# The second layer norm's scale and shift moved from ScalarE to GpSimd, beside a split of matrix operands on VectorE

## The chip, the cores and the metric

One core of one Trainium2 chip runs the whole program. The metric is the device time of one execution in microseconds, the median over several runs. The core's engines work side by side, each through its own list of instructions in order, and meet by semaphores: TensorE (PE; its weight loads are PEld), VectorE (DVE), ScalarE (ACT), GpSimd (POOL) and SyncE (SP, which here only issues DMAs).

## The reference, cut to what matters

The input `x` is 32 graphs of 256 nodes with 128 features. There are two residual blocks, each with a layer norm and a maximum with zero ahead of it:

```
h = jnp.maximum(_layernorm(x, axis=-1), 0.0)
x = x + _L0_gnn_ref(h, adj, W, a)                 # graph attention (GAT)
h = jnp.maximum(_layernorm(x, axis=-1), 0.0)      # the norm that the change is about
x = x + _L1_gnn_ref(h, adj, ...)                  # GCN, then LSTMs over windows of 1 to 4 nodes
...
# in _L1_gnn_ref
h = relu(einsum('ts,bsh->bth', adj, x @ Wg0 + bg0))
h = relu(einsum('ts,bsh->bth', adj, h @ Wg1 + bg1))
for p in range(1, 5):                             # LSTM over windows of p nodes
    last = _lstm_last(Wih[p-1], Whh[p-1], bih[p-1], bhh[p-1], windows of p nodes)
    h = h with node p*i + p-1 replaced by last[i]
```

All of it is float32. Layer norm is `(x - mean) / sqrt(var + 1e-5)` over the features. The kernel forms a scale and a shift for each node from the node's mean and variance, so that the norm is `x * scale + shift`.

## The kernel before, in words

The 32 graphs are worked as 16 pairs; a pair is 512 nodes, four tiles of 128 nodes (partitions) by 128 features. Everything stays in SBUF: `xs` holds all tiles.

There are three stages, each a software pipeline written out by hand. `ticks` runs a body once per tick and gives each step of the body its own pair (`live(s)` says whether step s has a pair in this tick).

Stage A (`phase_a`, 16 pairs) is the GAT. Stage B (`phase_b`) is the GCN and the LSTM for p = 1; its first four ticks run beside the last ticks of stage A. After it come the `ROUNDS`, the LSTMs for p = 2, 3 and 4, and the output.

In stage B, TensorE's products are exact float32 products made of three matmuls each: an operand is split in a high part (rounded to the type fp32r) and a low part (the rest), and `hi*hi + lo*hi + hi*lo` is summed (`product`, L1044). Each step therefore needs a split between two products: ScalarE writes the high part of what lies in PSUM (`part_hi`, L600), VectorE the low part (`part_lo`, L820 or L822). The steps of one pair are:

- step 0: the normed tile is written to `v_norm` by ScalarE (`second_norm`, L510: four activations with Relu, one per tile, scale and bias per node); VectorE splits it (`s_hi[0]` by a copy, L834, and `s_lo[0]` by a subtraction, L836).
- step 1: twelve matmuls with the adjacency matrix (`adjT`); step 2: four with `wg0` and the bias (the last is L1114); step 3: three with `wg1`; then ScalarE adds a bias (`y1`, L607) and TensorE turns the result with four transposes (`turned`, L1090) for step 4: twelve matmuls with `adjP`.
- step 5: nine matmuls for the three LSTM gates; ScalarE's sigmoids and tanh (L583, L576), VectorE's cell products (L796 to L807).

In one tick TensorE goes through steps 5, 4, 3, 2, the transposes, and 1. ScalarE goes through tanh, the gates I, G and O, `part_hi(4)`, `y1`, `part_hi(2)`, `part_hi(3)`, `second_norm`, `part_hi(1)`. The gate O waits until VectorE has read the row that it overwrites (L796). VectorE goes through L796, L800, L804, L807, `part_lo(4)`, `part_lo(2)`, `part_lo(3)`, the split of step 0 (L834, L836), `part_lo(1)`.

`second_norm(t)` may overwrite `v_norm` when VectorE has split the pair before (`b_lo[0]` at t). The first of them is issued in tick 16 of stage A, as soon as TensorE has turned the last tile of the first norm, which uses the same `v_norm`.

GpSimd computes the scales and shifts in chunks of 16 tiles (`norm_scale`, L407 to L416, whose power L415 is the longest instruction): four chunks for the second norm, each when VectorE has taken that chunk's statistics. Then it splits the LSTM weights for p = 2 to 4 in twelve pieces of two instructions each (`split_weights`, L474 and L475), one or two per tick: each piece waits for `one_lo`, VectorE's L807 in a tick of stage B. TensorE and ScalarE wait for all pieces (`wl_ok` at 2) before the LSTMs of p = 2.

Of the kernel before, what the change touches and what calls it, by code (L numbers as in the profile page):

```python
# [5 lines left out]
def preln_gat_gcn_lstm_kernel(  # L6
# [22 lines left out]
    fp32 = mybir.dt.float32  # L29
    fp32r = mybir.dt.float32r  # L30
    ALU = mybir.AluOpType
# [6 lines left out]
    PAIRS = B // 2  # L38
# [11 lines left out]
    SKIPS = 4  # L50
# [8 lines left out]
    with ctx:  # L59
# [7 lines left out]
        xs = sb("xs", [P, TILES, D])  # L67
# [314 lines left out]
        def _(pool):  # L382
# [88 lines left out]
            def split_weights(p, m, c):  # L471
                i, j = (p - 1) // 2, (p - 1) % 2
                g = slice(c * 2 * D, (c + 1) * 2 * D)
                done(nc.gpsimd.tensor_copy(wl_of[0][i][:, j, m, g], wraw[:, m, p - 1, g]))  # L474
                done(nc.gpsimd.tensor_tensor(wl_of[1][i][:, j, m, g], wraw[:, m, p - 1, g],  # L475
                                             wl_of[0][i][:, j, m, g].bitcast(fp32), ALU.subtract))
# [4 lines left out]
            split_weights(1, 0, 1)  # L481
            nc.gpsimd.nop().then_inc(wl_ok, 1)

            for c in range(4):
                pool.wait_ge(stats_ok, TILES + (c + 1) * QUARTER)
                norm_scale(1, c * QUARTER, QUARTER)


            for n_, (p, m, c) in enumerate((p, m, c) for p in range(2, SKIPS + 1) for m in range(2) for c in range(2)):
                pool.wait_ge(one_lo, 1 + 3 * n_ // 4)  # L490
                split_weights(p, m, c)
            nc.gpsimd.nop().then_inc(wl_ok, 1)

        @block.scalar
        def _(act):
# [56 lines left out]
                    nc.scalar.activation(pT[:, :, :].rearrange("p k i -> p (k i)"),  # L552
                                         psPT.rearrange("p b n -> p (b n)"), ACT.Copy).then_inc(a_pT, 1)

            def second_norm(t):
                act.wait_ge(ln_ok, t + (PAIRS + 1))
                normalise(1, t, range(4), b_v)

            def phase_a(t, ph, live):
                behind = (t - 1, ph - 1, lambda s: live(s + 1))  # L560
                early_a(*behind)
                first_norm(t, ph, live)
                if isinstance(t, int) and t == PAIRS:
                    act.wait_ge(a_T, PAIRS)
                    second_norm(0)
                late_a(*behind)
                if isinstance(t, int) and t == 4:
                    act.wait_ge(rs_ps, 1)
                    nc.scalar.activation(rs_raw[:, :], ps[:, 7, 0:N], ACT.Copy).then_inc(rs_read, 1)

            act.wait_ge(ones_ok, 1)
            def phase_b(t, ph, live):
                if live(6):

                    act.wait_ge(one_cell, t - 5)
                    nc.scalar.activation(one_row(R_TC), one_row(R_C), ACT.Tanh).then_inc(one_act, 1)  # L576
                if live(5):

                    for j, g in enumerate((I, G, O)):
                        act.wait_ge(one_gate, t * 3 + (j + 1 - 15))  # L580
                        if g == O:
                            after(act, one_h, t - 5, 0)
                        nc.scalar.activation(one_row(g), ps[:, 4 + g, :], ACT.Tanh if g == G else ACT.Sigmoid,  # L583
                                             bias=bl[:, g:g + 1]).then_inc(one_act, 1)

                def part_hi(s):
                    if not live(s):
                        return
                    if s == 4:
                        dst = h_hi[:, bass.ds((t - 4) * PN, PN)]  # L590
                    else:
                        dst = s_hi[:, s, :]
                    if s == 3:

                        act.wait_ge(b_T, t - 2)
                    else:
                        act.wait_ge(b_mm[s], t - s + 1)
                    if s < 4:
                        after(act, b_mm[s + 1], t - s, 0)
                    nc.scalar.activation(dst, ps[:, TURNED if s == 3 else s - 1, :],  # L600
                                         ACT.Copy if s in (1, 3) else ACT.Relu).then_inc(b_hi[s], 1)

                part_hi(4)
                if live(3):
                    act.wait_ge(b_mm[3], t - 2)
                    after(act, b_T, t - 3, 0)
                    nc.scalar.activation(y1[:, :], ps[:, 2, :], ACT.Identity, bias=b1_col[:, 0:1]).then_inc(b_y, 1)  # L607
                part_hi(2)
                part_hi(3)
                if live(0) and not (isinstance(t, int) and t == 0):  # L610

                    act.wait_ge(b_lo[0], t)
                    second_norm(t)
                part_hi(1)

            ticks(act, 5, 4, phase_a, beside=phase_b, lag=1)
# [52 lines left out]
        def _(dve):  # L669
# [115 lines left out]
            def phase_b(t, ph, live):  # L785
# [43 lines left out]
                if live(0):  # L829

                    v = v_norm[:, :, :].rearrange("p k f -> p (k f)")
                    dve.wait_ge(b_v, t + 1)
                    after(dve, b_mm[1], t, 0)
                    nc.vector.tensor_copy(s_hi[:, 0, :], v).then_inc(b_hi[0], 1)  # L834
                    dve.wait_ge(b_hi[0], t + 1)
                    nc.vector.tensor_tensor(s_lo[:, 0, :], v, s_hi[:, 0, :].bitcast(fp32),  # L836
                                            ALU.subtract).then_inc(b_lo[0], 1)
                part_lo(1)

            ticks(dve, 5, 4, phase_a, beside=phase_b)  # L840
# [412 lines left out]
```

## Time and profile before

| | us |
|---|---|
| median of 3 runs | 450.65 (450.28 to 450.68) |
| the profiled execution | 451.49 |
| span of its instructions | 449.5 |
| PE busy in the span | 426.2 (95%) |
| DVE busy | 376.1 (84%) |
| ACT busy | 333.6 (74%) |
| POOL busy | 67.3 (15%) |

The times are of whole executions; the span is that of the instructions of the one execution that the profiler recorded. Busy time adds up the instructions' own durations. A matmul's duration is longer than the distance to the next one, since matmuls are pipelined, so PE's idle time is read from the starts of neighbouring matmuls and from what the profile says they waited for. Stage A ends, beside the first ticks of stage B, at about 112 us of the span; stage B alone runs to about 226 us.

### The profile page before, as it was taken

The page shows a single profiled execution, that of the slowest core. Times are in us where ns is not written, and L with a number is a line of the kernel's source. Part 1 is how long each engine was busy: PE and PEld are TensorE (multiplying, and loading weights), DVE is VectorE, ACT ScalarE, POOL GpSimd, SP SyncE. Part 2 cuts the span into 40 slices and gives each one's busy share as a digit, 9 for nine tenths or more (in the row PEclk, how much of TensorE's full clock was granted, in tenths as well). Part 3 has the DMA queues.
Part 4 walks back from the last instruction along what each step waited for, and adds up shares of the span by engine and source line. Part 5 has one row for each costly group of instructions (what it writes and reads, how often), then busy time and mean ns, then how long its engine had stood idle before and what let it go on. Part 6 is the DMA issues. An engine that isn't in the chain of part 4 may idle for free.

```text
span 449.5 us, 7890 instructions
## 1 busy us (share of the span) xinstructions
PE 426.2 (95%) x2472; PEld 369.0 (82%) x2472; DVE 376.1 (84%) x994; ACT 333.6 (74%) x651; POOL 67.3 (15%) x145
## 2 busy tenths in 40 slices
PE   5689999979999999999999999999999999999995
PEld 4468788878888888888778888899999988887884
DVE  5999999987778787877778888878888789888995
ACT  3779999966899999897787768667767675574552
POOL 3678442240411313100000000000000000000000
PEclk9989999989999999999999999999999999999999
DMA  8910000000000000000000000000000000002116
GB/s 244 335 56 1 1 3 0 0 1 0 2 0 2 0 0 0 0 0 0 1 1 1 0 1 1 0 2 0 1 1 1 2 0 0 1 23 71 47 47 188
DMA packets 14212, 11.67 MB, mean 26 GB/s; under 512 B 1123, under 2 KB 12390, under 8 KB 13926
## 3 DMA queue, kind: packets, MB, share of 16 engines
q1 hardware_dynamic: 12118, 10.11, 7.5%
q10 hardware_dynamic: 2064, 1.18, 1.0%
q8 instruction: 16, 0.26, 0.2%
q14 instruction: 14, 0.11, 0.1%
HBM read 7.10 MB, written 4.19 MB: 25 GB/s over the span
## 4 chain that ended last, share of the span: by engine, by line
PE 69%; DVE 21%; ACT 4%; issue 3%; DMA 1%; DVEq 1%; POOL 0%; ACTq 0%; POOLq 0%
PE ps L1044 45%; PE ps L1188 12%; PE ps L1192 6%; DVE score L760 5%; DVE score L726 4%; DVE xs L774 3%; DVE stats L675 2%; PE ps L1090 2%; DVE stats L716 2%; ACT v_norm L510 1%; PE ps L1024 1%; ACT work L635 1%; PE ps L1135 1%; DMA xs<-in_x 1%; PE ps L1114 1%
## 5 line engine op out<-in xcount | busy, mean ns | idle before, releaser
L635 ACT ACTIVATE work<-ps,bl 128x512 f32<-128x512 f32 (+2 forms) x204 | 111.1, 628 | 26.9 <-PE ps L1192 19.3
L1044 PE MATMUL ps<-h_hi,wl_hi 128*128 128x512 f32 (+3 forms) x252 | 93.5, 371 | 0.9 <-DVE xs L916 0.8
L1044 PE MATMUL ps<-h_hi,wl_lo 128*128 128x512 f32 (+3 forms) x252 | 92.8, 368 | 0.0
L1044 PE MATMUL ps<-h_lo,wl_hi 128*128 128x512 f32 (+3 forms) x252 | 92.7, 368 | 0.0
L625 ACT ACTIVATE work<-work 128x512 f32<-128x512 f32 (+2 forms) x56 | 31.5, 571 | 45.1 <-DVE work L911 34.6
L510 ACT ACTIVATE v_norm<-xs,shift,scale 128x128 f32 (+1 forms) x128 | 52.7, 490 | 2.6 <-POOL shift L425 2.6
L1044 PEld LDWEIGHTS ps<-h_hi,wl_hi 128*128 128x128 f32 x252 | 47.5, 188 | 8.3 <-issue 1.2
L1044 PEld LDWEIGHTS ps<-h_lo,wl_hi 128*128 128x128 f32 x252 | 47.4, 188 | 6.6
L1044 PEld LDWEIGHTS ps<-h_hi,wl_lo 128*128 128x128 f32 x252 | 47.5, 188 | 5.6
L1188 PE MATMUL ps<-s_hi,wl_hi 128*128 128x512 f32 (+2 forms) x144 | 51.7, 362 | 0.0
L1188 PE MATMUL ps<-s_hi,wl_lo 128*128 128x512 f32 (+2 forms) x144 | 51.2, 358 | 0.0
L1024 PE MATMUL ps<-wh,pT 128*128 128x130 f32 x256 | 34.2, 288 | 2.4 <-DVE xs L774 2.1
L583 ACT ACTIVATE work<-ps,bl 128x512 f32<-128x512 f32 x48 | 30.9, 685 | 6.4 <-DVE work L796 5.1
L1024 PEld LDWEIGHTS ps<-wh,pT 128*128 128x128 f32 x256 | 31.4, 198 | 4.9 <-ACT pT L552 3.3
L1192 PE MATMUL ps<-s_lo,wl_hi 128*128 128x512 f32 (+2 forms) x144 | 34.4, 358 | 0.3 <-DVE s_lo L873 0.3
L600 ACT ACTIVATE s_hi<-ps 128x512 fp32r<-128x512 f32 x48 | 28.2, 593 | 5.5 <-PE ps L1114 2.1
L862 DVE TENSOR_TENSOR s_hi<-work 128x512 fp32r<-128x512 f32 (+2 forms) x36 | 22.0, 610 | 12.0 <-ACT work L625 11.1
L543 ACT ACTIVATE prob<-score,ebias 128x256 f32<-128x256 f32 x64 | 27.4, 512 | 5.7 <-DVE ebias L738 5.7
L866 DVE TENSOR_TENSOR work<-work 128x512 f32<-128x512 f32 (+2 forms) x52 | 31.3, 602 | 0.0
L1188 PEld LDWEIGHTS ps<-s_hi,wl_hi 128*128 128x128 f32 x144 | 27.1, 188 | 3.0
L1188 PEld LDWEIGHTS ps<-s_hi,wl_lo 128*128 128x128 f32 x144 | 27.1, 188 | 2.9
L1192 PEld LDWEIGHTS ps<-s_lo,wl_hi 128*128 128x128 f32 x144 | 25.4, 188 | 3.8 <-DVE s_lo L873 0.6
(136 smaller groups left out, 911.7 us busy)
## 6 DMA issues: line engine op xcount, KB each, us to landing
result<-xs SPq DMA_DIRECT2D x12, 256.0 KB, 2.3
work<-in_w_ih_t SPq DMA_DIRECT2D x1, 1024.0 KB, 10.4
work<-in_w_hh_t SPq DMA_DIRECT2D x1, 1024.0 KB, 9.4
xs<-in_x SPq DMA_DIRECT2D x2, 256.0 KB, 3.8
xs<-in_x SPq DMA_DIRECT2D x1, 512.0 KB, 7.2
result<-xs SPq DMA_DIRECT2D x4, 128.0 KB, 2.5
result<-xs ACTq DMA_DIRECT2D x4, 128.0 KB, 2.8
adj_raw<-in_adj ACTq DMA_DIRECT2D x1, 256.0 KB, 6.8
```

The lines of the kernel that those rows point to most:

```text
L510: ins = nc.scalar.activation(v_norm[:, k, :], xs[:, bass.ds(i, 1), :].rearrange("p o f -> p (o f)"), ACT.Relu, scale=scale[:, which, bass. ...
L543: ins = nc.scalar.activation(prob[:, m, k], score[:, m, k], ACT.Exp, scale=1.0 - SLOPE, bias=ebias[:, m, k:k + 1])
L583: nc.scalar.activation(one_row(g), ps[:, 4 + g, :], ACT.Tanh if g == G else ACT.Sigmoid, bias=bl[:, g:g + 1]).then_inc(one_act, 1)
L600: nc.scalar.activation(dst, ps[:, TURNED if s == 3 else s - 1, :], ACT.Copy if s in (1, 3) else ACT.Relu).then_inc(b_hi[s], 1)
L625: nc.scalar.activation(lw[:, par, R_TC, 0:cols], lw[:, par, R_C, 0:cols], ACT.Tanh).then_inc(c_act[par], 1)
L635: nc.scalar.activation(lw[:, par, g, 0:cols], ps[:, 4 * par + g, 0:cols], ACT.Tanh if g == G else ACT.Sigmoid, bias=bl[:, (p - 1) * GATES ...
L760: ins = nc.vector.scalar_tensor_tensor(score[:, m, k], psS[:, b * N:(b + 1) * N], wh[:, m, k, D + 1:D + 2], score[:, m, k], ALU.max, ALU.add)
L866: nc.vector.tensor_tensor(row(r, par, R_H), row(r, par, O), row(r, par, R_TC), ALU.mult).then_inc(c_h[par], 1)
L1024: ins = nc.tensor.matmul(psA[:, b, ui * (D + 2):(ui + 1) * (D + 2)], pT[:, 2 * b + uj, ui * P:(ui + 1) * P], wh[:, (ph - 4) % 4, 2 * b + u ...
L1044: ins = nc.tensor.matmul(dst, a, b, start=start and n_ == 0, stop=stop and n_ == 2)
L1188: nc.tensor.matmul(ps[:, 4 * par + g, 0:cols], part, s_hi[:, par, 0:cols], start=False, stop=False)
L1192: nc.tensor.matmul(ps[:, 4 * par + g, 0:cols], weights(p, 1, g)[0], s_lo[:, par, 0:cols], start=False, stop=True).then_inc(c_gate[par], 1)
```

## The change: what it does

The four activations of `second_norm` go from ScalarE's list to GpSimd's, as four `tensor_scalar` instructions (multiply by the scale, add the shift) without the maximum with zero. VectorE's split takes the maximum on: the copy (L834) becomes a `tensor_scalar` with a maximum, the subtraction (L836) a `scalar_tensor_tensor` that takes the maximum and then subtracts. GpSimd waits for the same two events as ScalarE did (the last transposes of the first norm for pair 0, `b_lo[0]` for the others), and for no scale but its own.

GpSimd's list changes its order with it: the first two chunks of scales, then the pairs' norms one by one, the third chunk after pair 4 and the fourth after pair 6; the twelve pieces of the LSTM weights follow the norms of pairs 7 to 15 (two after pairs 7, 10 and 13, one after the others), and their own waits for `one_lo` are gone.

```diff
@@ -481,14 +481,33 @@
             split_weights(1, 0, 1)
             nc.gpsimd.nop().then_inc(wl_ok, 1)
 
-            for c in range(4):
+            def second_scale(c):
                 pool.wait_ge(stats_ok, TILES + (c + 1) * QUARTER)
                 norm_scale(1, c * QUARTER, QUARTER)
 
-            for n_, (p, m, c) in enumerate((p, m, c) for p in range(2, SKIPS + 1) for m in range(2) for c in range(2)):
-                pool.wait_ge(one_lo, 1 + 3 * n_ // 4)
-                split_weights(p, m, c)
+            def second_norm(q):
+                if q == 0:
+                    pool.wait_ge(a_T, PAIRS)
+                else:
+                    pool.wait_ge(b_lo[0], q)
+                for k in range(4):
+                    i = q * 4 + k
+                    ins = nc.gpsimd.tensor_scalar(v_norm[:, k, :], xs[:, i, :], scale[:, 1, i:i + 1], shift[:, 1, i:i + 1],
+                                                  ALU.mult, ALU.add)
+                ins.then_inc(b_v, 1)
+            second_scale(0)
+            second_scale(1)
+            pieces = [(p, m, c) for p in range(2, SKIPS + 1) for m in range(2) for c in range(2)]
+            for q in range(PAIRS):
+                second_norm(q)
+                if q in (4, 6):
+                    second_scale(q // 2)
+                for n_, piece in enumerate(pieces):
+                    if 7 + 3 * n_ // 4 == q:
+                        split_weights(*piece)
             nc.gpsimd.nop().then_inc(wl_ok, 1)
 
         @block.scalar
@@ -552,17 +571,10 @@
                     nc.scalar.activation(pT[:, :, :].rearrange("p k i -> p (k i)"),
                                          psPT.rearrange("p b n -> p (b n)"), ACT.Copy).then_inc(a_pT, 1)
 
-            def second_norm(t):
-                act.wait_ge(ln_ok, t + (PAIRS + 1))
-                normalise(1, t, range(4), b_v)
             def phase_a(t, ph, live):
                 behind = (t - 1, ph - 1, lambda s: live(s + 1))
                 early_a(*behind)
                 first_norm(t, ph, live)
-                if isinstance(t, int) and t == PAIRS:
-                    act.wait_ge(a_T, PAIRS)
-                    second_norm(0)
                 late_a(*behind)
                 if isinstance(t, int) and t == 4:
                     act.wait_ge(rs_ps, 1)
@@ -607,10 +619,6 @@
                     nc.scalar.activation(y1[:, :], ps[:, 2, :], ACT.Identity, bias=b1_col[:, 0:1]).then_inc(b_y, 1)
                 part_hi(2)
                 part_hi(3)
-                if live(0) and not (isinstance(t, int) and t == 0):
-                    act.wait_ge(b_lo[0], t)
-                    second_norm(t)
                 part_hi(1)
 
             ticks(act, 5, 4, phase_a, beside=phase_b, lag=1)
@@ -831,10 +839,10 @@
                     v = v_norm[:, :, :].rearrange("p k f -> p (k f)")
                     dve.wait_ge(b_v, t + 1)
                     after(dve, b_mm[1], t, 0)
-                    nc.vector.tensor_copy(s_hi[:, 0, :], v).then_inc(b_hi[0], 1)
+                    nc.vector.tensor_scalar(s_hi[:, 0, :], v, 0.0, None, ALU.max).then_inc(b_hi[0], 1)
                     dve.wait_ge(b_hi[0], t + 1)
-                    nc.vector.tensor_tensor(s_lo[:, 0, :], v, s_hi[:, 0, :].bitcast(fp32),
-                                            ALU.subtract).then_inc(b_lo[0], 1)
+                    nc.vector.scalar_tensor_tensor(s_lo[:, 0, :], v, 0.0, s_hi[:, 0, :].bitcast(fp32), ALU.max,
+                                                   ALU.subtract).then_inc(b_lo[0], 1)
                 part_lo(1)
 
             ticks(dve, 5, 4, phase_a, beside=phase_b)
```

## Rows read from the trace of the kernel before

**Rows 1.** Windows: length; busy us (instructions) of PE, PEld, DVE, ACT, POOL; clock.
```profile
84.30:89.30 5.00, 5.00 (x40) 4.34 (x39) 5.00 (x24) 5.00 (x13) 0.00 (x0) 1.00 0.00 0
...
132.74:205.31 72.57, 72.21 (x441) 61.85 (x441) 59.95 (x121) 66.42 (x131) 13.57 (x24) 1.00 0.00 0
205.31:212.38 7.07, 7.07 (x44) 6.18 (x45) 5.49 (x11) 5.33 (x9) 0.00 (x0) 1.00 0.00 0
```

**Rows 2.** Chain that ended last, 84 to 130 us: start, us, what.
```profile
107.58 1.65 ACT v_norm L510 x4
...
119.08 1.65 ACT v_norm L510 x4
```

**Rows 3.** Timeline of PE, first ticks of stage B: start, duration, what [idle before].
```profile
105.87 0.47 PE L1044 MATMUL ps<-s_hi,wg_hi 128*128 128x512 f32 x1 [0.38 <-issue]
...
110.58 0.40 PE L1044 MATMUL ps<-s_lo,wg_hi 128*128 128x512 f32 x1
111.16 0.47 PE L1044 MATMUL ps<-s_hi,wg_hi 128*128 128x512 f32 x1 [0.18 <-DVE s_lo L820]
...
116.34 0.39 PE L1044 MATMUL ps<-s_lo,wg_hi 128*128 128x512 f32 x1
116.90 0.47 PE L1044 MATMUL ps<-s_hi,wg_hi 128*128 128x512 f32 x1 [0.17 <-DVE s_lo L820]
...
124.67 0.40 PE L1114 MATMUL ps<-rs_parts,b_parts 128*128 128x512 f32 x1
125.49 0.66 PE L1090 MATMUL ps<-ident,y 128*128 128x128 f32 x4 [0.42 <-ACT y L607]
```

**Rows 4.** Timeline around the transposes, in a tick with and one without second_norm.
```profile
146.50 0.69 ACT L607 ACTIVATE y<-ps,b_col 128x512 f32<-128x512 f32 x1
146.82 0.40 PE L1114 MATMUL ps<-rs_parts,b_parts 128*128 128x512 f32 x1
147.25 0.66 PE L1090 MATMUL ps<-ident,y 128*128 128x128 f32 x4
...
211.63 0.69 ACT L607 ACTIVATE y<-ps,b_col 128x512 f32<-128x512 f32 x1
212.13 0.40 PE L1114 MATMUL ps<-rs_parts,b_parts 128*128 128x512 f32 x1
212.38 0.66 PE L1090 MATMUL ps<-ident,y 128*128 128x128 f32 x4
```

**Rows 5.** Groups on POOL by line and shape: busy us, mean ns.
```profile
L475 POOL TENSOR_TENSOR wl_lo<-work,wl_hi 128x256 fp32r<-128x256 f32 x14 | 10.3, 739 | 1.1
L474 POOL CAST wl_hi<-work 128x256 fp32r<-128x256 f32 x14 | 5.6, 398 | 54.6 <-DVE h_lo L807 54.2 <-POOL adjP_lo L466 0.2
L411 POOL TENSOR_SCALAR ln_d<-ln_d 128x16 f32<-128x16 f32 x7 | 1.9, 271 | 0.4
...
L448 POOL CAST ident_r<-ident 128x128 fp32r<-128x128 f32 x1 | 0.3, 291 | 0.0
```

**Rows 6.** Timeline of DVE in a steady tick of stage B.
```profile
150.11 0.43 DVE L834 CAST s_hi<-v_norm 128x512 fp32r<-128x512 f32 x1 [0.85 <-ACT v_norm L510]
150.58 0.69 DVE L836 TENSOR_TENSOR s_lo<-v_norm,s_hi 128x512 fp32r<-128x512 f32 x1
...
151.79 0.82 DVE L796 TENSOR_TENSOR work<-work 128x176 f32<-128x176 f32 x3
```

**Rows 7.** Timeline of ACT in the same tick, gate O.
```profile
152.70 0.69 ACT L583 ACTIVATE work<-ps,bl 128x512 f32<-128x512 f32 x1 [0.46 <-DVE work L796]
```

**Rows 8.** Timelines of DVE and POOL where their instructions overlap.
```profile
97.06 0.69 DVE L836 TENSOR_TENSOR s_lo<-v_norm,s_hi 128x512 fp32r<-128x512 f32 x1
97.15 0.67 POOL L411 TENSOR_SCALAR ln_d<-ln_d 128x16 f32<-128x16 f32 x1
...
119.72 2.91 POOL L415 TENSOR_TENSOR scale<-ln_a,half 128x16 f32<-128x16 f32 x1
121.22 0.69 DVE L836 TENSOR_TENSOR s_lo<-v_norm,s_hi 128x512 fp32r<-128x512 f32 x1
```

## The prediction

> **What bounds the kernel now.** I read the windows first, then the chain of waits, then the timelines of TensorE, ScalarE and VectorE around what the chain named.
>
> In the windows [rows 1] the reader is to see who is full where. In stage A alone VectorE is: 5.00 of 5.00 us of a tick. In stage B TensorE is: 72.21 of 72.57 us in ten ticks, while ScalarE has 66.42 and VectorE 59.95. The first window takes part of this change off ScalarE at no gain: the norm of pair 0 is issued there, and VectorE sets that pace.
>
> The three windows also hold an experiment that the old kernel makes by itself. A steady tick takes 72.57 / 10 = 7.257 us. The tick of 205.31 to 212.38 does the same 44 matmuls but has no norm left to do, since its pair would be the seventeenth: 7.07 us. The difference is 0.18 us. It sits in one place [rows 4]: with the norm, the transposes (L1090) start 147.25 - 146.82 = 0.43 us after the matmul before them, without it 212.38 - 212.13 = 0.25 us. What they wait for is `y` (L607), which starts 0.32 us ahead of that matmul with the norm and 0.50 us ahead without.
>
> In the first ticks of stage B the norm is on the chain itself [rows 2]: 1.65 us in each of three ticks (first and last are shown, the third is at 113.33). TensorE, though, stands still for much less than that there, because it still has stage A's matmuls to fill in [rows 3].
>
> **The change, part by part.**
>
> *Off ScalarE.* Four activations in each of 16 pairs go, 1.65 us per pair [rows 2], about 26 us of ScalarE in all. As ScalarE is not full, only what TensorE waits for counts.
>
> First ticks: TensorE's stalls that hang on the norm [rows 3]. At 105.87 it had stood 0.38 us; the low part that it wants comes from VectorE behind the split, which sat waiting for the norm. At 111.16 it starts 0.58 us after the matmul before, at 116.90 0.56 us after; with 0.25 us for an unhindered distance (the one of the free tick [rows 4]) that is 0.33 and 0.31 us lost, both on the same low part. At 125.49 the distance is 0.82 us, so 0.57 lost, on `y`, in the tick in which ScalarE has to do the norm, a table load and three gates one after the other. Sum: 0.38 + 0.33 + 0.31 + 0.57 = 1.6 us. What is late next there is TensorE itself: without these stalls its matmuls follow each other.
>
> Steady ticks: from the transposes at 125.49 [rows 3] to those at 205.31 [rows 1] are 79.82 us, 11 ticks of 7.256. Each can fall to 7.07: 11 x 0.18 = 2.0 us. What comes next is TensorE again, and a tick cannot go below its own matmuls.
>
> Does VectorE let `y` come earlier? The free tick had no split to do, the changed ticks still have, so VectorE's dates have to be looked at. The split (L834) now sits idle 0.85 us for the norm [rows 6]; L796 follows it in order, and gate O, which waits 0.46 us for L796 [rows 7], is followed by `part_hi(4)` and `y`. So if GpSimd's norm is there in time, L796 and O move up by as much as 0.85 us, where `y` needs 0.18. VectorE may lose 0.85 - 0.18 = 0.67 us ahead of L796 before the first of the gain is gone.
>
> *On GpSimd.* Four `tensor_scalar` of 128x128 with a scalar per partition. The trace has none of them. Below: the one-input copy of the same size, 0.29 us; above: the two-input subtraction of twice the size, 0.74 us [rows 5]. I take 0.3, by the nearest in size and number of inputs; a norm is then 1.2 us, at the upper end 3.0 us. It starts when the split (L836) of the pair before ends, 150.58 + 0.69 = 151.27 in the tick shown, and is wanted at the next tick's split, 7.07 us after 150.11 - 0.85 = 149.26 [rows 6], thus at 156.33: 5.1 us of room. Even 3.0 us fit, so the cost is nothing on the path; cover ends at 1.27 us per instruction. Pair 0's norm falls into stage A, and its split is reached only just ahead of 97.06 [rows 8].
>
> *Scales in between.* A chunk is 2.91 us [rows 8] and nine small instructions of 0.27 (L411's mean [rows 5], which includes slow ones), so 5.3 us. It runs behind the norms of pairs 4 and 6, whose successors then start at most some 1.2 + 5.3 = 6.5 us after the last, under a tick: nothing on the path.
>
> *Weight pieces.* A piece is 0.398 + 0.739 = 1.14 us [rows 5], twelve of them in nine ticks, now behind the norm: 1.2 + 1.14 = 2.3 us, or 3.5 with two. Both are under a tick, and the last is done behind pair 15's norm, some five ticks ahead of the LSTMs that wait for it. No DMA is moved, and no queue is passed by one.
>
> *VectorE's split.* The copy at 0.43 us becomes a `tensor_scalar`; bounds are that and the 0.69 us of the two-input form [rows 6]; I take 0.43, as it has still one tensor input. The subtraction stays at 0.69, with the same inputs. At the upper bound VectorE does 0.26 us more per tick and has 7.07 - 59.95 / 10 = 1.07 idle, and 0.67 ahead of L796: nothing either way.
>
> *What GpSimd and VectorE do to each other.* This is the unknown. Until now GpSimd's pieces ran where VectorE reads PSUM; now norm and pieces run behind L836, into the row L796, L800, L804, L807, all from SBUF: 0.82 + 0.43 + 0.69 + 0.69 = 2.6 us, the last three by their likes in [rows 6]. The trace has two such meetings [rows 8]. L411, issued 0.09 us after L836, took 0.67 us instead of its mean of 0.27 [rows 5]: GpSimd waited. And L836 at 121.22, 1.5 us into a GpSimd instruction of 2.91, took its 0.69 us as everywhere: VectorE did not wait. So I take nothing for VectorE and up to the whole row, 2.6 us, for GpSimd: norm plus that is 3.8 of the 5.1 us of room. The other bound, VectorE waiting for all of it, is the second rival.
>
> The Trainium skill, "SBUF — State Buffer", section "SBUF: two separate sides", says that the two engines share a port pair under an exclusive lock: whichever instruction starts first holds it to its end, and the other is blocked fully. The first meeting agrees; the second speaks against it, as L836 would have had to wait until 119.72 + 2.91 = 122.63, though that instruction reads only 16 columns. By the rule the sum would be the second rival's.
>
> **Sum.** 1.6 + 2.0 = 3.6 us. The profiled execution took 451.49 us, span 449.5 and 1.99 around it: 445.9 and 447.9 after. It lay 0.84 above the median of the runs; on the median, 450.65 - 3.6 = 447.05, so **447.0**. Nothing behind 212 us is touched, so the gain is handed on to the end.
>
> **Rivals.**
>
> 1. *Only the first ticks gain.* VectorE or GpSimd's port costs some 0.2 to 0.8 us ahead of L796, `y` stays as late as it was, and the steady ticks stay at 7.26. For it: VectorE's row has little air before L796. Against: 0.67 us are free. Time: 450.65 - 1.6 = 449.05.
>
> 2. *VectorE is held up by GpSimd and becomes the bound (slower).* Place: the nine ticks with weight pieces. Of the norm's four instructions the first two fall beside `part_lo(1)`, which reads PSUM; the other two and the piece hold the port against VectorE for 0.6 + 1.14 = 1.74 us, with two pieces 2.88. VectorE has 1.07 free per tick at the new pace, so six ticks lengthen by 0.67 and three by 1.81: 9.4 us, against 3.6 gained: 456.5 at the full hold. It decides from about 70% of these durations, where the loss is 6 x 0.15 + 3 x 0.95 = 3.7 and eats the gain; under 37% nothing is lost. Half-way between 70 and 100% it is 6 x 0.41 + 3 x 1.38 = 6.6 lost: 453.7. For it: the norm runs just where VectorE reads two SBUF operands. Against: the second meeting in [rows 8]. The rule of the Trainium skill's page "SBUF — State Buffer" named above comes to this rival.
>
> 3. *No difference.* GpSimd's norm is late, above 1.27 us per instruction or with its waits on VectorE, and VectorE waits at the split as before, for another engine: about 450.6. For it: that instruction isn't in the trace. Against: it would have to be four times its nearest row.
>
> **How the numbers follow.** The forecast has 0.60, with its own range of 446.2 to 447.7 (the stalls of [rows 3] may come back in part, the small ones beside them may go too). Rival 1 has 0.18, rival 2 0.14, rival 3 0.08. About 0.2%, 0.9 us, is what a measurement of this kernel can tell from no change. Faster: 0.60 + 0.18 = 0.78; same 0.08; slower 0.14. The range goes from 446.0 to 450.2, which takes in rival 1 and partial forms of the others.
>
> **What would show it.** Right: the transposes of stage B 0.25 us behind the matmul before them and ticks of 7.07; L834 without idle time for the norm; `tensor_scalar` on GpSimd near 0.3 us, longer where it lies beside L796 to L807; stage B's first transposes of a full tick (125.49) some 1.6 us earlier. Wrong: L796, L804, L807 longer than now or with idle time that ends with GpSimd; ticks with two pieces longer than ticks with one; L834 still waiting, now for GpSimd; or the `tensor_scalar` on VectorE at 0.69 us.

## The result, and the profile after

The changed kernel's median is 445.79 us (444.55 to 446.20, 5 runs); the kernel before had 450.28 us beside it (448.84 to 450.68). The ratio is 0.9895 (95% interval 0.9871 to 0.9919): faster by about 1%. The forecast was 447.0 us in a range of 446.0 to 450.2: right in direction, and the median lies 0.2 us below the range.

The profiled execution took 444.66 us. Its span of 442.9 is 6.6 us less than that of the profiled execution before. That is more than the medians differ by (4.5 us), so the 6.6 us are taken apart first. Lines of the changed kernel are eight higher from the edit on: L1052 was L1044, L1098 (the transposes) L1090, L1122 L1114, L496 is GpSimd's norm, L842 and L844 are the split. Kernels of the experiments have their own line numbers; the names of the tiles tell which instruction a line is.

Windows of the changed kernel, columns as in [rows 1]: a tick of stage A alone, one tick of stage B, then ten.

```profile
84.30:89.30 5.00, 5.00 (x41) 4.34 (x40) 5.00 (x25) 4.47 (x10) 1.75 (x4) 1.00 0.00 0
...
114.02:121.10 7.08, 7.08 (x46) 6.19 (x45) 4.39 (x7) 5.97 (x9) 6.45 (x13) 1.00 0.01 2
...
128.17:198.90 70.73, 70.73 (x441) 61.87 (x441) 60.82 (x120) 53.64 (x90) 47.92 (x69) 1.00 0.00 0
```

The ten ticks take 70.73 us against 72.57 in [rows 1], with the same 441 matmuls, and TensorE is now busy in all of it. ScalarE went from 66.42 to 53.64, GpSimd from 13.57 to 47.92. In stage A VectorE is still the full one: ScalarE's release there bought nothing.

TensorE's timeline in the first ticks of stage B, to be laid beside [rows 3]. The distance from one start to the next is what counts.

```profile
101.86 1.04 PE L1044 MATMUL ps<-ident,prob 128*128 128x128 f32 x8
102.65 0.48 PE L1052 MATMUL ps<-s_hi,wg_hi 128*128 128x512 f32 x1
...
107.35 0.40 PE L1052 MATMUL ps<-s_lo,wg_hi 128*128 128x512 f32 x1
107.58 0.40 PE L1052 MATMUL ps<-s_hi,wg_hi 128*128 128x512 f32 x1
...
110.40 0.28 PE L1052 MATMUL ps<-adjT_lo,s_hi 128*128 128x256 f32 x1
110.73 0.35 PE L1052 MATMUL ps<-adjP_hi,s_hi 128*128 128x256 f32 x1
...
112.70 0.39 PE L1052 MATMUL ps<-s_lo,wg_hi 128*128 128x512 f32 x1
112.93 0.40 PE L1052 MATMUL ps<-s_hi,wg_hi 128*128 128x512 f32 x1
...
120.70 0.40 PE L1122 MATMUL ps<-rs_parts,b_parts 128*128 128x512 f32 x1
120.95 0.66 PE L1098 MATMUL ps<-ident,y 128*128 128x128 f32 x4
```

Three rows of the kernel before that [rows 3] did not have are needed beside it:

```profile
104.46 1.04 PE L1036 MATMUL ps<-ident,prob 128*128 128x128 f32 x8
...
113.91 0.28 PE L1044 MATMUL ps<-adjT_lo,s_hi 128*128 128x256 f32 x1
114.37 0.36 PE L1044 MATMUL ps<-adjP_hi,s_hi 128*128 128x256 f32 x1 [0.19 <-issue]
```

All the stalls are gone or smaller. From the eight transposes to the next matmul: 1.41 us before (104.46 to 105.87), 0.79 now. Then 0.58 became 0.23, 0.46 became 0.33, 0.56 became 0.23, and the 0.82 ahead of the transposes became 0.25.

VectorE and ScalarE in one steady tick, beside [rows 6] and [rows 7]:

```profile
144.36 0.43 DVE L842 TENSOR_SCALAR s_hi<-v_norm 128x512 fp32r<-128x512 f32 x1
144.82 0.69 DVE L844 SCALAR_TENSOR_TENSOR s_lo<-v_norm,s_hi 128x512 fp32r<-128x512 f32 x1
145.43 0.68 DVE L828 TENSOR_TENSOR s_lo<-ps,s_hi 128x512 fp32r<-128x512 f32 x1
146.03 0.82 DVE L804 TENSOR_TENSOR work<-work 128x176 f32<-128x176 f32 x3
147.00 0.44 DVE L808 CAST h_hi<-work 128x512 f32 x1
147.37 0.68 DVE L812 TENSOR_TENSOR work<-work 128x512 f32<-128x512 f32 x1
147.97 0.77 DVE L815 TENSOR_TENSOR h_lo<-work,h_hi 128x512 f32 x1
...
146.95 0.69 ACT L595 ACTIVATE work<-ps,bl 128x512 f32<-128x512 f32 x1 [0.38 <-DVE work L804]
```

The split no longer waits, and its new forms cost what the old ones did, 0.43 and 0.69 us. GpSimd in the same tick:

```profile
145.69 3.38 POOL L496 TENSOR_SCALAR v_norm<-xs,scale,shift 128x128 f32<-128x128 f32 x4 [2.02 <-DVE s_lo L844]
149.02 0.39 POOL L474 CAST wl_hi<-work 128x256 fp32r<-128x256 f32 x1
```

Four instructions of 0.45 us take 1.75 us where nothing delays them (the norm that starts at 101.59); here they take 3.38. The first runs while VectorE reads PSUM (L828). A later one waits: over all 64 of them the shortest takes 447 ns, the longest 1685. Behind the two chunks of scales the next norm starts 7.15 and 9.08 us after the norm before (112.04 to 119.19 and 124.40 to 133.48), and still no steady tick of this execution is longer than 7.08.

**Where the 6.6 us came from.** Two pieces of it are not the change's. The first, before stage B: VectorE's L738, which has two small SBUF inputs and takes 0.16 us, took 1.42 in the profiled execution before, while GpSimd's placing copies ran back to back. In the chain that ended last it is a piece of 1.34 us.

```profile
46.04 1.34 DVE ebias L738
```

```profile
45.70 1.66 POOL L465 CAST adjP_lo<-adjT_lo 128x84 fp32r<-128x84 f32 x6
47.30 0.20 POOL L466 CAST adjP_lo<-adjT_lo 128x8 fp32r<-128x8 f32 x1
...
45.96 1.42 DVE L738 SCALAR_TENSOR_TENSOR ebias<-m,low 128x4 f32<-128x4 f32 x1
```

In the changed kernel's execution the same instruction (L746) met the same copies and took 0.16 us:

```profile
45.92 0.16 DVE L746 SCALAR_TENSOR_TENSOR ebias<-m,low 128x4 f32<-128x4 f32 x1
```

GpSimd's program up to there is the same in both kernels, and the instruction came 0.26 us into the series of copies in both executions; what decided between 1.42 and 0.16 us is open. The stall left 0.94 us: the sixteen matmuls behind the wait between the stages start at 96.84 before and at 95.90 after. The second is the speed of these sixteen matmuls. The chain of the kernel before, then of the changed one:

```profile
96.84 3.60 PE ps L1024 x16
```

```profile
95.90 2.03 PE ps L1032 x16
```

TensorE had stood for 2 us waiting for VectorE in both. Before, its granted clock from 98 to 100 us was 0.50, the lower of its two levels; after, 1.00. That is 1.57 us. From there on the rest: to the transposes at 125.49 [rows 3] and 120.95, 25.05 against 23.02 us, so 2.03; from these to the transposes at 205.31 and 198.74, 11 ticks in 79.82 against 77.79, so 2.03 again. 0.94 + 1.57 + 2.03 + 2.03 = 6.57. The first 2.03 still holds a little of the clock: in the chains the eight transposes behind the sixteen matmuls (L1036, now L1044) take 0.95 us before and 0.87 after, and before, the granted clock from 100 to 102 us was 0.88.

So the theory tested was: the change's own gain is 4.06 us, in TensorE's waits (theory A), and the other 2.5 us belong to single executions of either kernel (C). The rival (B): the change itself keeps the clock up between the stages.

### The profile page after: what moved, and what is told of

It reads as the page before. It is cut to its first block, busy times and chain, and to the rows that moved or that the text cites. A ratio compares the mean times of both kernels' runs of the same rounds, so it can differ in the third digit from the quotient of the medians.

```text
span 442.9 us, 7799 instructions
## 1 busy us (share of the span) xinstructions
PE 422.6 (95%) x2472; PEld 368.1 (83%) x2472; DVE 375.8 (85%) x994; ACT 312.5 (71%) x587; POOL 110.7 (25%) x209
## 4 chain that ended last, share of the span: by engine, by line
PE 78%; DVE 15%; issue 2%; ACT 2%; DMA 1%; DVEq 1%; ACTq 0%
PE ps L1052 48%; PE ps L1196 12%; PE ps L1200 6%; DVE score L768 4%; DVE score L734 3%; PE ps L1032 3%; DVE stats L683 2%; PE ps L1098 2%; DVE xs L782 1%; PE ps L1007 1%; PE ps L1044 1%; ACT work L643 1%; DVE stats L724 1%; PE ps L1143 1%; PE ps L1122 1%
## 5 line engine op out<-in xcount | busy, mean ns | idle before, releaser
L1052 PE MATMUL ps<-h_hi,wl_hi 128*128 128x512 f32 (+3 forms) x252 | 93.5, 371 | 0.9 <-DVE xs L924 0.8
L1052 PE MATMUL ps<-h_hi,wl_lo 128*128 128x512 f32 (+3 forms) x252 | 92.8, 368 | 0.0
L1052 PE MATMUL ps<-h_lo,wl_hi 128*128 128x512 f32 (+3 forms) x252 | 92.7, 368 | 0.0
L496 POOL TENSOR_SCALAR v_norm<-xs,scale,shift 128x128 f32<-128x128 f32 x64 | 44.0, 701 | 42.8 <-DVE s_lo L844 36.4
L1052 PEld LDWEIGHTS ps<-h_hi,wl_hi 128*128 128x128 f32 x252 | 47.5, 188 | 8.3 <-issue 1.2
L1052 PEld LDWEIGHTS ps<-h_lo,wl_hi 128*128 128x128 f32 x252 | 47.4, 188 | 6.6
L1052 PEld LDWEIGHTS ps<-h_hi,wl_lo 128*128 128x128 f32 x252 | 47.5, 188 | 5.6
L1032 PE MATMUL ps<-wh,pT 128*128 128x130 f32 x256 | 32.6, 280 | 2.4 <-DVE xs L782 2.3
L1032 PEld LDWEIGHTS ps<-wh,pT 128*128 128x128 f32 x256 | 29.9, 190 | 5.1 <-issue 2.5
```

The lines of the kernel that those rows point to most:

```text
L496: ins = nc.gpsimd.tensor_scalar(v_norm[:, k, :], xs[:, i, :], scale[:, 1, i:i + 1], shift[:, 1, i:i + 1], ALU.mult, ALU.add)
L1032: ins = nc.tensor.matmul(psA[:, b, ui * (D + 2):(ui + 1) * (D + 2)], pT[:, 2 * b + uj, ui * P:(ui + 1) * P], wh[:, (ph - 4) % 4, 2 * b + u ...
L1052: ins = nc.tensor.matmul(dst, a, b, start=start and n_ == 0, stop=stop and n_ == 2)
```

## The experiments

Ratios are to the kernel before, timed on the same chip in the same comparison. Its 30 executions in the first set of four went from 448.63 to 453.03 us, median 449.99.

**The changed kernel again.** No edit.

> The changed kernel as it is, once more. Theory A (the gain is TensorE's waits: 1.6 to 2.0 us in the first ticks of stage B and 11 x 0.18 = 2.0 us in the steady ticks): 3.6 to 4.0 us under the kernel before, ratio 0.991 to 0.992. Theory B (a further gain belongs to the change: TensorE keeps its clock where stage A hands over to stage B, 1.57 us in the two traces): about 5.2 us, ratio 0.988, with a granted clock near 1.00 in that stretch in this profile too. Theory C (what lay beyond 4.0 us in the first comparison is the scatter of single executions, a clock dip of 1.6 us and a stall of VectorE of 0.9 us that either kernel can have): a ratio between the two, and executions of either kernel that lie 1 to 2 us apart.

446.14 us (444.40 to 447.81), ratio 0.9903 (0.9869 to 0.9936). The interval takes in all three theories; the trace decides. This profiled execution of the changed kernel has both disturbances that the first had not. Its VectorE timeline, and its chain:

```profile
45.65 1.42 DVE L746 SCALAR_TENSOR_TENSOR ebias<-m,low 128x4 f32<-128x4 f32 x1
```

```profile
96.51 2.59 PE ps L1032 x16
```

So B falls: the changed kernel too loses its clock there in some executions, and stalls at L746 in some. Nor does the change make the undisturbed executions clearly more frequent: within 1 us of the fastest lie 5 of 12 executions of the changed kernel and 31 of 81 of the kernel before, over all comparisons. The fastest executions, 444.40 and 448.63, are 4.2 us apart.

**The first five pairs' norms alone on GpSimd; the last eleven alone.**

```diff
 # first five: GpSimd
-            for q in range(PAIRS):
-                second_norm(q)
+            for q in range(5):
+                second_norm(q)
 # and ScalarE, ahead of part_hi(1)
+                if live(0) and not (isinstance(t, int) and t < 5):
+                    act.wait_ge(b_lo[0], t)
+                    second_norm(t)
...
 # last eleven: GpSimd
-            for q in range(PAIRS):
+            for q in range(5, PAIRS):
                 second_norm(q)
 # and ScalarE does pairs 0 to 4 as before
```

The chunks of scales run together here: the last two behind the five norms in the first variant, all four ahead of the norms in the second.

> Only the norms of pairs 0 to 4 are on GpSimd, the others on ScalarE as before, weight pieces with their old waits. Theory A: the stalls of the first ticks go, the steady ticks stay at 7.25 us: 1.6 to 2.0 us under the kernel before. Theory B: this variant has the whole of the clock's gain too: 3.5 us. If only the steady ticks mattered: no gain.

> The norms of pairs 0 to 4 are on ScalarE as before, those of pairs 5 to 15 on GpSimd with the weight pieces behind them. Theory A: ticks of 7.07 us, 11 x 0.18 = 2.0 us under the kernel before, and the transposes at the old distance up to pair 4. Theory B: the same 2.0, no clock gain. The rival in which GpSimd takes the SBUF port from VectorE: ticks of 7.07 us in the ticks without weight pieces only, a gain under 1 us.

First five: 447.05 us (446.33 to 449.30), ratio 0.9942 (0.9921 to 0.9963). Last eleven: 446.74 us (446.35 to 449.00), ratio 0.9940 (0.9918 to 0.9961). Each is about half of the gain, 2.3 us by the fastest executions, a little more than was expected; by the medians, which scatter, it is 2.9 and 3.3. The traces separate the two terms. The sixteen matmuls and the transposes of the first full tick, in first five and then in last eleven:

```profile
95.67 2.03 PE ps L1040 x16
120.72 0.66 PE L1106 MATMUL ps<-ident,y 128*128 128x128 f32 x4
```

```profile
95.77 2.03 PE ps L1041 x16
122.77 0.66 PE L1107 MATMUL ps<-ident,y 128*128 128x128 f32 x4 [0.42 <-ACT y L624]
```

From start to start these are 25.05 us, as in the changed kernel, and 27.00. The steady ticks behind them take 7.25 us in first five and 7.07 in last eleven. Both parts of the forecast's sum are there and add up, and the piece behind the norm does not eat the second.

**VectorE's part alone.**

```diff
-  xs[...], ACT.Relu, scale=..., bias=...)            # ScalarE, both norms
+  xs[...], ACT.Relu if which == 0 else ACT.Identity, scale=..., bias=...)
-  nc.vector.tensor_copy(s_hi[:, 0, :], v)
+  nc.vector.tensor_scalar(s_hi[:, 0, :], v, 0.0, None, ALU.max)
-  nc.vector.tensor_tensor(s_lo[:, 0, :], v, s_hi..., ALU.subtract)
+  nc.vector.scalar_tensor_tensor(s_lo[:, 0, :], v, 0.0, s_hi..., ALU.max, ALU.subtract)
```

> All norms on ScalarE, but without the maximum, which VectorE's split takes: VectorE's part of the change alone. Theory A: no difference, within 0.2 us, and L834's and L836's successors at 0.43 and 0.69 us. If the split's forms were the dearer ones, 0.26 us more per tick on VectorE: up to 3 us slower, since the split lies between the norm and the low part that TensorE waits for in the first ticks.

449.82 us (448.62 to 453.02), ratio 0.9995 (0.9973 to 1.0017). The fastest executions, 448.62 and 448.63, are the same, and the split's two instructions take 0.43 and 0.69 us in this profile too: no cost of the maximum can be seen.

**No norm at all.**

```diff
-                for k in range(4):
-                    ins = nc.gpsimd.tensor_scalar(v_norm[:, k, :], xs[:, i, :], ...)
-                ins.then_inc(b_v, 1)
+                nc.gpsimd.nop().then_inc(b_v, 1)
```

> The changed kernel with the second norm's 64 GpSimd instructions left out (the split takes what lies in v_norm); the waits and the weight pieces stay. Theory A: no faster than the changed kernel, within 0.3 us: ticks of 7.07 us either way, since TensorE is full. If GpSimd's norm cost time by the SBUF port or by being late, this one is faster by that much.

447.14 us (446.34 to 448.95), ratio 0.9933 (0.9909 to 0.9956): with less work it is slower than the changed kernel, by 1.9 us by the fastest executions. Theory A's expectation, no faster, held, but it did not expect slower. The spans of the profiled executions differ by 1.7 us, and by the transposes 1.3 of it lie in the nine ticks with weight pieces: 7.13 to 7.15 us with one piece, 7.34 to 7.39 with two. The rest lies ahead of the sixteen matmuls, where other kernels' profiles scatter too. VectorE and GpSimd in a tick with one weight piece:

```profile
146.33 0.68 DVE L824 TENSOR_TENSOR s_lo<-ps,s_hi 128x512 fp32r<-128x512 f32 x1
146.93 1.37 DVE L800 TENSOR_TENSOR work<-work 128x176 f32<-128x176 f32 x3
...
146.57 0.40 POOL L474 CAST wl_hi<-work 128x256 fp32r<-128x256 f32 x1 [5.84 <-DVE s_lo L840]
147.04 0.82 POOL L475 TENSOR_TENSOR wl_lo<-work,wl_hi 128x256 fp32r<-128x256 f32 x1
```

Without the norm ahead of it the piece's copy is under way when VectorE comes to L800 (L796 of [rows 6]), and its three instructions take 1.37 us instead of 0.82. VectorE is held up after all.

**The norm twice and three times.**

```diff
-                for k in range(4):
+                for k_ in range(4 * 2):        # 4 * 3 in the other
+                    k = k_ % 4
...
+                    if k_ % 4 == 3 and k_ + 1 < 4 * 2:
+                        done(ins)
```

> Each pair's norm computed twice on GpSimd, the second time over the first: eight instructions of 0.45 us, 3.6 us, in the 5.1 us that the prediction gave it. Theory A: as fast as the changed kernel, within 0.3 us, if GpSimd yields the port. The rival of the prediction, VectorE held up: with twice the hold the ticks lengthen where pieces and norm together hold over 1.07 us: 3 us slower than the changed kernel or more, with longer L804, L812, L815.

> Three times over: twelve instructions, 5.4 us and their waits on VectorE, above the 5.1 us. Theory A: VectorE's split waits for GpSimd, the ticks go back to 7.25 us and beyond; with 1.14 us of a weight piece per tick GpSimd has 6.6 us of work in a tick of 7.07 and 7.7 where two fall: 2 to 8 us slower than the changed kernel. If the room were wider than the prediction said: no difference.

Twice: 454.67 us (452.94 to 455.42), ratio 1.0092 (1.0067 to 1.0118). Three times: 481.41 us (479.41 to 483.12), ratio 1.0699 (1.0670 to 1.0729). Both expectations failed: against the median of the changed kernel run again, twice was expected to be free and costs 8.5 us, three times was expected to cost 2 to 8 and costs 35.3. VectorE's split, and the norms of pairs 7 and 8, with twice:

```profile
141.60 0.59 DVE L846 TENSOR_SCALAR s_hi<-v_norm 128x512 fp32r<-128x512 f32 x1 [2.67 <-POOL v_norm L498]
...
137.96 3.61 POOL L498 TENSOR_SCALAR v_norm<-xs,scale,shift 128x128 f32<-128x128 f32 x8
144.50 5.09 POOL L498 TENSOR_SCALAR v_norm<-xs,scale,shift 128x128 f32<-128x128 f32 x8
```

The eight instructions are 3.6 us by themselves and take 5.09 with their waits on VectorE. The longest wait of the split, 2.67 us, is for the norm of pair 7, which starts only at 137.96 because the fourth chunk of scales is ahead of it. Most of the loss is there: the three ticks around the two chunks and the two pieces behind them take 8.80, 10.28 and 8.62 us, together 6.5 more than three ticks of 7.07. The other ticks with pieces lose 1.9 in all: 7.07 to 7.18 us behind one piece, 7.60 behind two. The split's subtraction, 0.95 us on average in stage B instead of 0.70, shows VectorE held up as well; the run does not tell how much of the loss is that and how much the late norm. The cover that the forecast gave the norm, up to 1.27 us per instruction, is gone at 0.9 behind a chunk or two pieces.

**The clock between the stages.**

```diff
+                if isinstance(t, int) and t == PAIRS + 1:
+                    for k in range(16):
+                        nc.tensor.transpose(ps[:, 0, (k % 4) * P:(k % 4 + 1) * P], ident[:, :], ident[:, :])
                 if live(4):
```

> The changed kernel with 16 transposes of the identity, into a bank that is free then, just where TensorE waits 2 us for VectorE between stages A and B. Theory C: the clock dip behind that wait, which single executions of either kernel have (16 matmuls of L1024's kind in 3.6 or 2.6 us instead of 2.03), is gone in all executions, and the spread of the times narrows by up to 1.6 us at its upper end; the fastest executions stay at 444.4. If the dip has another cause, the same executions as before: 444.4 to 447.8.

445.51 us (444.71 to 446.52), ratio 0.9889 (0.9864 to 0.9914). In its profile TensorE is busy through the wait, and the sixteen matmuls behind it run at full clock:

```profile
94.78 1.91 PE L1025 MATMUL ps<-ident 128*128 128x128 f32 x16
97.06 2.03 PE L1035 MATMUL ps<-wh,pT 128*128 128x130 f32 x16 [0.37 <-DVE xs L782]
```

The upper end came down by 1.3 us. Six executions, one of them profiled, are too few to show that the dip is gone for good. The sixteen matmuls start 1.16 us later here than in the first profile of the changed kernel, though no L746 took more than 0.28 us: the length of stage A scatters for another reason too, which stays open.

**The placing copies moved, alone and with the transposes, and both in the kernel before.**

```diff
             for part, placed in ((adjT_hi, adjP_hi), (adjT_lo, adjP_lo)):
+                pool.wait_ge(a_bias, 7 if part is adjT_hi else 8)
```

> The changed kernel with GpSimd's 14 placing copies of adjP (L465, L466) put right behind VectorE's L738 of two later ticks, so that no L734 or L738 falls into their back-to-back series. Theory C: the stall of L738 (1.42 us instead of 0.16 in some executions of either kernel) is gone in all executions, and with it 0.9 us of the spread; the fastest stay at 444.4, the clock dip's 1.6 us remain in some. If the stall had another cause, executions 0.9 us apart stay.

> The changed kernel with both: the placing copies behind L738 and the 16 transposes that keep TensorE going between the stages. Theory C: all executions near the fastest of the changed kernel, 444.4 to 445.2, median about 444.8, which is 5 us under the kernel before and 1 us under the changed one.

> The same two edits in the kernel before, the norm still on ScalarE. Theory C: its executions draw together at the low end too, 448.6 to 449.4, median about 448.9; then the change's own gain is the difference to the kernel with both edits and the norm on GpSimd: 2.0 + 2.0 = 4.0 to 4.2 us. Theory B: the kernel before keeps its dips for another reason, and its median stays near 450.

Moved: 444.92 us (444.42 to 446.93), ratio 0.9900 (0.9873 to 0.9927). With the transposes: 445.06 us (444.43 to 446.36), ratio 0.9899 (0.9874 to 0.9925). Both in the kernel before: 449.06 us (448.70 to 451.06), ratio 0.9993 (0.9975 to 1.0010). In all three profiles the longest L738 is 0.18 us. With the copies moved alone, the profiled execution (446.93) has its sixteen matmuls in 3.68 us: the clock dip comes without the stall, as was expected. The sixteen matmuls of the last two, changed kernel first, and the transposes of their first full tick:

```profile
96.11 2.03 PE ps L1036 x16
121.16 0.66 PE L1102 MATMUL ps<-ident,y 128*128 128x128 f32 x4
```

```profile
96.10 2.03 PE ps L1028 x16
123.09 0.66 PE L1094 MATMUL ps<-ident,y 128*128 128x128 f32 x4 [0.42 <-ACT y L608]
```

This pair is the cleanest measure of the change: 449.06 - 445.06 = 4.0 us by the medians, 3.8 by the spans, 447.0 and 443.2. Of the 3.8 the first ticks have 26.99 - 25.05 = 1.94, without the clock's part, and the 11 steady ticks 79.81 - 77.97 = 1.84. One tick of the changed kernel, behind a chunk of scales and two pieces, takes 7.24 us here instead of 7.07: the split's subtraction runs beside a piece and takes 1.11 us. The same tick is 7.17 in the profile of the changed kernel run again, and 7.07 or 7.08 in the first one and with either edit alone.

The execution times draw together, but not wholly. Of the changed kernel's six, one of 446.36 us remains, at a granted clock of 0.996; of the twelve of the kernel before, three lie above 449.5 (449.95, 450.52 and 451.06), against eight of seventeen without the edits, and the median, 449.06 against 449.17 beside it, is no different. What disturbs these is open. Neither edit makes a version that is clearly faster than the changed kernel.

**The weight pieces ahead of the norm.** The same work in the other order.

```diff
                     pool.wait_ge(b_lo[0], q)
+                for n_, piece in enumerate(pieces):
+                    if 7 + 3 * n_ // 4 == q:
+                        split_weights(*piece)
                 for k in range(4):
...
-                for n_, piece in enumerate(pieces):
-                    if 7 + 3 * n_ // 4 == q:
-                        split_weights(*piece)
```

> The changed kernel with GpSimd's order turned in the nine ticks with weight pieces: behind the same wait the pieces come first, then the pair's norm. The work is the same. If the port goes to who is there first (reading of the no-norm kernel): the piece's copy and subtraction are under way when VectorE comes to L804, whose three take 1.37 us or more instead of 0.82, `y` is late again, the nine ticks take 7.13 to 7.4 us, and the kernel is 0.5 to 2.5 us slower than the changed one: 446 to 448, and more where the norm is late behind two pieces. If VectorE always went first: 7.07 us per tick and no difference.

447.73 us (447.02 to 449.82), ratio 0.9958 (0.9939 to 0.9976): 2.6 us slower than the changed kernel by the fastest executions. VectorE, GpSimd, and the transposes of TensorE in one tick:

```profile
138.92 0.43 DVE L843 TENSOR_SCALAR s_hi<-v_norm 128x512 fp32r<-128x512 f32 x1 [1.20 <-POOL v_norm L501]
...
139.99 0.68 DVE L829 TENSOR_TENSOR s_lo<-ps,s_hi 128x512 fp32r<-128x512 f32 x1
140.59 1.39 DVE L805 TENSOR_TENSOR work<-work 128x176 f32<-128x176 f32 x3
...
140.14 0.40 POOL L474 CAST wl_hi<-work 128x256 fp32r<-128x256 f32 x1 [1.25 <-DVE s_lo L845]
140.62 0.89 POOL L475 TENSOR_TENSOR wl_lo<-work,wl_hi 128x256 fp32r<-128x256 f32 x1
...
143.88 0.66 PE L1099 MATMUL ps<-ident,y 128*128 128x128 f32 x4 [1.13 <-ACT y L620]
```

The piece begins at 140.14, VectorE's L805 at 140.59, and L805 takes 1.39 us: VectorE waits for the piece that was there first. Eight such series of L805 take 1.39 to 1.58 us instead of 0.82. And behind a chunk of scales and two pieces the norm of pair 7 is late for the split, 1.20 us here. The two make about equal parts of the 2.3 us that stage B's ticks lost in this profile: this one tick takes 8.35 us, 1.28 more than 7.07, most of it the late norm; the next seven take 7.16 to 7.35, together 1.0 more.

## Why the prediction was right, and where it was wrong

The mechanism was right: TensorE's waits went, in the two places named. The time came out 1.26 us below the forecast. Of this 0.46 is the sum, 3.6 against 4.06 in the two traces, nearly all of it in the first ticks; 0.37 is that the kernel before had 450.28 beside the changed one and not 450.65; and 0.43 is that the two medians differ by 4.49, more than the traces' 4.06.

- **Stage A, no gain:** right. VectorE has 5.00 of 5.00 us there before and after.
- **First ticks, 1.6 us:** the mechanism was right, the term too small; it measured 2.03 in the first two traces and 1.94 in the pair with both edits. The step that failed is "At 105.87 it had stood 0.38 us". That number is the idle time in brackets, which counts from the modelled end of the matmul before. By starts the stall was 1.41 - 0.79 = 0.62 us. The others were read by starts and came out as read: 0.35, 0.33 and 0.57, against 0.33, 0.31 and 0.57. Another, at 114.37, was left out (0.13). These five make 2.00; what differs from the measured sum, under 0.1 us either way, is in the matmuls next to the stalls and in the clock ahead of them.
- **Steady ticks, 2.0 us:** right, 11 ticks at 7.072 instead of 7.256. The tick that the kernel before ran without a norm [rows 4] gave this to 0.01 us.
- **GpSimd's price, 0.3 us per instruction:** it measured 0.45 alone, within the bounds, and up to 1.69 with its waits. Hidden in this kernel. "Even 3.0 us fit" was not run, but the room of 5.1 us was too wide a reading: it left out that GpSimd waits for VectorE inside it and that pieces or scales may still be running. At 3.6 us the norm takes 5.1 with its waits, and it fits behind one piece (ticks of 7.07 to 7.18) but not behind two or behind a chunk.
- **Scales in between, nothing on the path:** right, with less room than was read. The norms behind the two chunks start 7.15 and 9.08 us after the norm before, not 6.5, and the kernel with the norm twice loses most of its time there.
- **Nothing for VectorE:** nearly right in this order (0.10 and 0.17 us in one tick, in two of the profiled executions), wrong as a rule. "The trace has two such meetings" was the failure: it had a third, L738 at 45.96, and that one showed VectorE held for 1.26 us by a series of GpSimd copies. It stood in the chain of waits as a piece of 1.34 us, in stage A, of which the prediction took no row for this. The meeting from which it took nothing, the power at 119.72, did not stand for copies and weight pieces. The second rival's mechanism is real. What keeps it out is the order: the norm's first instruction falls beside L828, which reads PSUM, VectorE's series of L804 to L815 then comes in first, and the pieces end up behind that series. That the three L804 take 0.82 us in the tick shown, and 1.37 or 1.39 with a piece ahead, is what the runs showed of it. The Trainium skill, "SBUF — State Buffer", section "Who interferes with whom", says that the order of issue decides who blocks; the last experiment agrees, with 1.39 to 1.58 us in eight ticks. Not every meeting does: L836 took its 0.69 us within the power of 2.91 [rows 8], and L746 its 0.16 within the series of copies.
- **The range:** its low end, 446.0, was the forecast less 1.0. Some 0.4 of this was used up by the first term. The rest went because the median of three runs, 450.65, was taken for the kernel's time to a few tenths: single executions of the kernel before lie between 448.6 and 453.0 us, those of the changed one between 444.4 and 447.8, and medians of a few of them move by over half a us. For the same reason 0.9 us was too fine a mark for what a few runs can tell.

## What to carry to other kernels

Read a stall of TensorE from the starts of neighbouring matmuls, in the kernel's own undisturbed repeats, not from the idle time in brackets: that understated the first stall here by 0.24 of 0.62 us. When work goes to GpSimd, its place in VectorE's order counts as well as its length: here first beside a VectorE instruction that reads PSUM, the long pieces last. Before a range is made, look through the whole chain of waits for single instructions far above their median, since they tell what executions differ by.

## What the runs showed that I had not expected

A series of GpSimd instructions that follow each other without a gap can hold VectorE for the whole series, not for one of them: L738 came in 0.26 us into six copies of 0.33 us and was done only when the last had ended, 1.42 us. It did so in three of the profiled executions; in the first of the changed kernel it took 0.16 at the same place. A kernel can lose time by doing less: without the 64 norm instructions it was 1.9 us slower, and 1.3 us could be read in the ticks where the weight pieces came 3 us earlier and met VectorE first.
